# A layer norm's variance from one square of the whole tile on ScalarE, summed by VectorE

## The reference

```
def _layernorm(x, axis=-1, eps=1e-05):
    m = jnp.mean(x, axis=axis, keepdims=True)
    v = jnp.var(x, axis=axis, keepdims=True)
    return (x - m) / jnp.sqrt(v + eps)
...
h = _L0_tok_ref(x, ...)                       # convolution, 16 taps, 64 -> 64: 735 tokens
h = h + _L0_attn_ref(_layernorm(h), Wq, Wk)   # softmax(q k^T / 8) applied to the normed input
h = h + _L0_ffn_ref(_layernorm(h), ...)       # 16 experts, top 2, hidden 128;
                                              # ends in a layer norm with gamma and beta
```

## Time and profile before

| | |
|---|---|
| median of 3 runs | 476.7 us (476.16 to 478.5) |
| the profiled execution, own time | 475.88 us |
| its span, first to last instruction | 474.0 us |
| TensorE busy | 418.6 us, 88% of the span |
| VectorE busy | 308.5 us, 65% |
| ScalarE busy | 164.5 us, 35% |
| GpSimd busy | 140.7 us, 30% |
| mean granted TensorE clock | 0.956 of full speed |

### The profile page before, as it was taken

How to read it: one execution, slowest core, us unless ns; L and a number is a source line. 1 busy time by engine, 2 the same in 40 slices (tenths; PEclk the granted TensorE clock), 3 DMA queues, 4 the chain that set the end, 5 groups by cost and what they waited for, 6 DMA issues and landing times.

```text
span 474.0 us, 7344 instructions
## 1 busy us (share of the span) xinstructions
PE 418.6 (88%) x2317; PEld 251.1 (53%) x2317; DVE 308.5 (65%) x681; ACT 164.5 (35%) x518; POOL 140.7 (30%) x153
## 2 busy tenths in 40 slices
PE   2839968999999998999999998999899889976991
PEld 1326544655656555665565555655565547543540
DVE  6029456785778567775777577856776677563661
ACT  2134541433344333532452334433362224132021
POOL 3010120104307142524424430724061533064201
PEclk9966968999999999999999999999999899998996
DMA  4801001930077005900193009600670039003900
GB/s 104 152 0 34 1 2 44 381 122 1 5 291 254 17 2 176 367 19 3 59 402 100 0 6 342 208 5 0 229 285 18 1 124 396 9 2 145 385 0 16
DMA packets 42707, 55.80 MB, mean 118 GB/s; under 512 B 23976, under 2 KB 26040, under 8 KB 42680
## 3 DMA queue, kind: packets, MB, share of 16 engines
q1 hardware_dynamic: 42680, 55.46, 34.2%
HBM read 53.57 MB, written 1.88 MB: 117 GB/s over the span
## 4 chain that ended last, share of the span: by engine, by line
PE 64%; DVE 16%; DMA 7%; ACT 5%; issue 5%; POOL 1%; DVEq 0%; POOLq 0%; SPq 0%; ACTq 0%
PE up L939 17%; PE wide L939 14%; PE mix L939 14%; PE small L939 10%; DMA gates_all<-gates_far 5%; DVE row_max L750 3%; DVE hidden L836 3%; DVE prob_sum L761 2%; PE wide L976 2%; DMA gates_far<-gates_t 2%; PE wide L1043 2%; PE small L969 1%; DVE keys L687 1%; ACT cen_sq L511 1%; DVE xn L700 1%
## 5 line engine op out<-in xcount | busy, mean ns | idle before, releaser
L836 DVE SCALAR_TENSOR_TENSOR hidden<-up,b_neg,gates_all 128x368 f32<-128x368 f32 x208 | 115.0, 594 | 45.6 <-PE up L939 34.2
L939 PE MATMUL up<-x,w_hi 128*128 128x368 f32 x256 | 97.7, 381 | 8.0 <-DVE hidden L836 7.0
L939 PE MATMUL mix<-hidden,w2s 128*64 128x368 f32 x512 | 104.2, 498 | 0.0
L939 PE MATMUL up<-x,w_lo 128*128 128x368 f32 x256 | 85.2, 333 | 0.0
L420 POOL TENSOR_SCALAR var_eps<-var 128x6 f32<-128x6 f32 x24 | 5.8, 241 | 250.1 <-ACT cen_sq L511 250.1
L939 PEld LDWEIGHTS up<-x,w_hi 128*128 128x128 f32 x256 | 48.8, 191 | 44.5 <-DVE hidden L836 21.4
L310 POOL TENSOR_TENSOR hidden<-relu,gates_all 128x368 f32<-128x368 f32 x42 | 44.5, 1089 | 40.4 <-ACT relu L552 26.1
L750 DVE TENSOR_REDUCE row_max<-wide 128x1 f32<-128x736 f32 (+1 forms) x48 | 42.9, 918 | 13.4 <-PE wide L939 12.9
L939 PEld LDWEIGHTS up<-x,w_lo 128*128 128x128 f32 x256 | 49.2, 192 | 0.0
L560 ACT ACTIVATE probs<-wide 128x736 f32<-128x736 f32 (+2 forms) x48 | 35.2, 785 | 27.7 <-PE wide L939 27.0
L939 PEld LDWEIGHTS mix<-hidden,w2s 128*64 128x64 f32 x512 | 27.6, 136 | 31.5 <-issue 29.7
(11 more groups left out here) (147 smaller groups left out, 492.1 us busy)
## 6 DMA issues: line engine op xcount, KB each, us to landing
gates_all<-gates_far SPq DMA_DIRECT2D x128, 368.0 KB, 8.0
xx<-x SPq DMA_DIRECT2D x16, 160.0 KB
w_raw<-L_ffn_w SPq DMA_DIRECT2D x2, 512.0 KB, 5.4
out<-outs SPq DMA_DIRECT2D x16, 64.0 KB
w2s<-L_ffn_w SPq DMA_DIRECT2D x1, 512.0 KB, 7.4
gates_far<-gates_t SPq DMA_DIRECT2D x8, 46.0 KB, 1.7
gates_all<-L_tok_w_real SPq DMA_DIRECT2D x1, 256.0 KB, 3.5
gates_all<-L_tok_w_imag SPq DMA_DIRECT2D x1, 256.0 KB, 4.2
```

The costliest lines, as they stand in the source:

```text
L836: dve.scalar_tensor_tensor(hidden[:, e % HIDDEN, s, :], up[s][:, 0:HALF], b1_neg[:, e:e + 1], gates_all[:, e, s * HALF:(s + 1) * HALF], AL ...
L939: return pe.matmul(dst, lhsT, rhs, start=start, stop=stop, skip_group_check=True)
```

## The change

ScalarE's `variance` becomes one square of the whole 128 x 384 tile, without an accumulator; it counts a new semaphore `s_sq[k]`. A new VectorE function `sum_squares` waits for it, adds up each row of 64 squares into `var[k]` and counts `s_var[k]`, on which GpSimd waits as before. `sum_squares` is called at these places of VectorE's queue: in an iteration behind expert 0's work (layer norm 2), expert 3's (layer norm 0) and expert 9's (layer norm 1); in the opening and at the start directly ahead of the normalisation; at the end behind the last centring. Within an expert's step it stands behind `hide`, `reduce_max`, `centre` and `add_probabilities` and ahead of `normalise`.

```diff
+        s_sq = [sem(f"ln{k}_squared") for k in range(3)]
...
             def variance(k, src, n):
 
                 act.wait_ge(s_cen[k], n + 1 + (CREDIT if k == 2 else 0))
-                for t in range(NT):
-                    last = act.activation(cen_sq[k][:, t, :], src[:, t, :], ACT.Square, scale=D ** -0.5,
-                                          accum_out=var[k][:, t:t + 1])
-                last.then_inc(s_var[k], 1)
+                act.activation(cen_sq[k][:], src[:], ACT.Square, scale=D ** -0.5).then_inc(s_sq[k], 1)
...
+            def sum_squares(k, n):
+                dve.wait_ge(s_sq[k], n + 1)
+                dve.tensor_reduce(var[k][:], cen_sq[k][:], AX.X, ALU.add).then_inc(s_var[k], 1)
...
             centre(0, 0)
+            sum_squares(0, 0)
             normalise(0, xn1[0], cen0[0], 0)
...
                     if att and e == 5:
                         add_probabilities(i, 4)
                         add_probabilities(i, 5)
+                    if not first and e == 0:
+                        sum_squares(2, i - 2)
+                    if conv and e == 3:
+                        sum_squares(0, i + 1)
+                    if att and e == 9:
+                        sum_squares(1, i)
                     if conv and e == 4:
                         normalise(0, xn1[1 - par], cen0[1 - par], i + 1)
...
                 scale_attention(0)
                 centre_sum(0, 0)
+                sum_squares(0, 1)
                 normalise(0, xn1[1], cen0[1], 1)
                 keys_lo(1)
+                sum_squares(1, 0)
                 normalise(1, xn2[0], cen1, 0)
                 query_lo(1)
...
+            sum_squares(2, BATCH - 1)
             dve.wait_ge(s_rstd[2], BATCH)
```

## The result

The changed kernel took 482.53 us (median of 4 runs, 481.74 to 483.65); the kernel before took 477.6 us beside it (median of 4, 476.16 to 478.73). The ratio is 1.0107, with a 95% interval of 1.0068 to 1.0146: slower by about 5 us. The profiled execution took 482.40 us with a span of 480.5 us, 6.5 us more than the span of before.

The account below looks back on a forecast made before the run. TensorE was taken as the bound, busy 49.47 of 50.70 us per steady iteration. Terms -0.88 + 5.4 + 2.7 + 0 - 0.2 = +7.0 us gave 483.3 us, range 479.8 to 486.3.

Parts of the forecast that it names:

- Opening, +5.4: Before iteration 1: sums right ahead of their normalisations make VectorE wait for rstd; +5.4 us, bounds 4.8 to 6.4.
- First and last variance, -0.88: At start and end, where the variance chain alone is exposed: 0.44 us shorter each, together -0.88.
- Push at expert 0, +2.7 to the end: Layer norm 2's sum delays expert 1's hidden product; TensorE 0.45 us later in each of iterations 2 to 7, +2.7.
- VectorE's stretch from expert 4 on (246.21, started by TensorE) shifts along: Step within expert 0's push: TensorE's delay of 0.45 us carries on into VectorE's later work, so nothing absorbs it.
- Sum at expert 3, 0: Layer norm 0's steady sum falls into VectorE's 1.07 us idle time; later GpSimd and SBUF sharing also taken as zero.
- the bounds that I gave: For GpSimd and VectorE slowing each other over SBUF after expert 3's sum: -0.63 to +0.70 us in each of five iterations.
- The forecast's own range: 480.6 to 486.0 us, chance 0.66; from the opening, the push and half of the sharing's bounds, -1.6 and +1.2.
- Layer norm 1, -0.1 each: Sum at expert 9 behind the hidden product lets GpSimd start slightly earlier; counts in iterations 6 and 7, -0.1 us each.
- The condition that I had named as its failure: The prediction fails if iterations stay at 50.7 us (51.1 expected), or if iteration 1 starts less than 4 us late.

Follow-up runs that it names:

- push_only: Kernel before with only layer norm 2's steady variance changed: one square, sum on VectorE at expert 0; 480.51 against 476.77 us, ratio 1.0068.
- ln0_only: Kernel before with only layer norm 0's steady variance changed: one square, sum on VectorE at expert 3; 474.48 against 476.77 us, ratio 0.9946.
- pool_late: Kernel before with only one more GpSimd wait, for expert 4's first hidden half, ahead of layer norm 0's eps and power; 474.25 against 476.9 us, ratio 0.9928.
- gamma_late: Changed kernel with opening sums earlier, layer norm 2's at expert 2, GpSimd's gamma and beta after the last sum of probabilities; 470.31 us, ratio 0.9881.

## Why the prediction was right

The time lay in the range and the direction was right. The steps:

- **Opening, +5.4.** Right in its mechanism, step for step: sums at 60.62 and 67.39 (forecast 60.91 and 67.58, less the 0.3 by which this run was early there), 1.9 us of waiting behind each, transposes 5.37 us late, 1.49 us for the first ones at the low clock. In size: the four openings with waiting sums average 50.97 us, the four with the old order (before, push_only, ln0_only, pool_late) 45.98 us: 5.0 us. The single pair of profiles has 6.5, since the granted clock stayed low longer in the one and came back early in the other. Openings with the same order of instructions differ by up to 1.9 us among these, and by 2.5 among the three with the sums moved ahead (44.43 to 46.96).
- **First and last variance, -0.88.** Right: -0.44 at the start. At the end the centring starts at 471.19 and the final product at 474.86, 3.67 us, where it was 4.10 (464.26 to 468.36): -0.43.
- **Push at expert 0, +2.7 to the end.** The push was sized rightly, 0.44 against 0.45 us, and by itself it goes through (push_only). The step that failed is "VectorE's stretch from expert 4 on (246.21, started by TensorE) shifts along": the stretch became 0.46 us shorter in the same kernel, TensorE's wait of 0.34 us behind it went, and +0.19 us were left over five iterations. Iteration 7, which has no such stretch, kept its push: TensorE was 6.60 us late at the transposes of the maxima and 7.07 at those of the attention's output behind them, a push of 0.47. On the size of one push: the instruction behind the sum starts 0.46 us after it (244.87 to 245.33), not 0.54. The prediction read this overlap as speaking against the Trainium skill, "VectorE: DVE Perf Modes", section "The DRAIN you can't avoid"; it left out that the same section says that a next instruction which is not held starts earlier, and the overlap agrees with that.
- **Sum at expert 3, 0.** The failed term behind it. The sum itself costs nothing, as said, but its effect on GpSimd was taken as zero by comparing 4.15 with 4.22 us for three instructions, the normalisation and the two last sums of probabilities, in iterations 4 and 6. Both rows are from the kernel before; where the sum puts GpSimd the same three take 3.69 us (0.96 + 2.73), and TensorE had been waiting for what stands behind them. The term measured -2.05 us (ln0_only). It was inside the bounds that I gave, -0.63 to +0.70 for each iteration. The forecast's own range has +1.2 for half of the upper bounds, where 5 x 0.70 / 2 makes 1.75 us; nothing measured came near either.
- **Layer norm 1, -0.1 each.** In iteration 7 from the hidden product at 420.96 to GpSimd's start at 422.72 are 1.76 us, against 1.85 (413.90 to 415.75): -0.09. Right, by iteration 7.

The terms as measured in the parts, opening 5.0, first and last -0.9, push and sharing +0.2, iteration 7's push +0.5, layer norm 1 -0.2, give +4.6 us, beside a measured 1.0107 x 477.6 - 477.6 = 5.1. The forecast of +7.0 was too high by some 2.0 us of the push that the sharing gave back in five iterations and by 0.4 in the opening. The condition that I had named as its failure, iterations that stay at 50.7 us, came true for this step: from the keys' projection of iteration 1 to that of iteration 6 they average 50.87 us, against 50.83 before. The opening, right by its mechanism, carried the direction. That the time came within 0.8 us of the 483.3 is in part luck: the kernel before ran at 477.6 us beside it and not at 476.7, which hides 0.9 us of what the forecast had too much.

## What to carry to other kernels

A sum that moves to another engine's in-order queue costs by what stands right behind it there, not by its 0.54 us: ahead of its own consumer it exposed the whole chain of 1.9 us through GpSimd, twice, and a few places earlier, with the same instructions, it was free. Before a push is carried to the end of an iteration, look for work that runs on both VectorE and GpSimd over SBUF behind it: a shift of one against the other can give back as much as the push took. And with two effects of equal size and opposite sign in one change, the whole tells nothing of either; here one part alone made the kernel 0.5% faster and the other 0.7% slower. They show when each is run alone, and in a stretch that leaves out what varies from one execution to the next.

## What the runs showed of the hardware

VectorE's normalisation (two SBUF inputs, 768 elements) took 0.95 to 0.96 us beside GpSimd's small passes and 1.58 us where GpSimd's large passes had begun ahead of it. Beside VectorE's long instructions, in turn, GpSimd's small passes of 128 x 6 elements grew from 0.24 to 0.80 us and from 1.35 to 1.99 us, as the timeline of the changed kernel shows. Which of the two began first went with which was lengthened: the power at 247.15 us in the kernel before, begun 0.08 us ahead of VectorE's sums of probabilities, kept its 1.35 us, and these sums took 1.87 us, as the two last ones did in gamma_late, where no large pass lay beside them. The Trainium skill, "GPSIMD Engine Reference", section "Specifications", says that the SBUF interfaces are shared with VectorE and contended when a VectorE instruction has two SBUF inputs; the rows agree. What I had not expected is that a wait added on GpSimd alone, at no other place, makes this kernel 0.7% faster.

The granted clock in the opening varied between executions of the same instruction order: between 74 and 78 us it was 1.00 in the kernel before and 0.79 in pool_late, with nothing changed ahead of that. Openings of that order took 45.01 to 46.87 us, so one pair of profiles can't tell a difference of 1 us there.
